# Two buffers for unpacked weights, the down unit's split one quad later on VectorE, and a four-step unpacking, in the first sweep of a 4-bit feed-forward kernel

## What is computed

```
x = layernorm(x + attention(x, w_qkv, w_o))      # 16 heads, causal
gate = x Wg^T ; up = x Wu^T                       # 4096 columns each
out  = (gelu(gate) * up) Wd^T
x = layernorm(x + out)
```

## Time and profile before

| | |
|---|---|
| median of 3 runs | 3083.97 us (3083.12 to 3085.64) |
| the profiled execution, its own time | 3093.57 us |
| its span, first to last instruction | 3091.8 us |
| PE busy, share of the span | 91% |
| DVE, ACT, POOL busy | 55%, 41%, 33% |
| mean granted TensorE clock | 0.961 of full speed |
| feed-forward phase | from about 911 us to the end |
| its first sweep | from about 937 us to about 1577 us |

### The profile page before, as it was taken

One profiled execution on the slowest core, in us unless ns is written; L12 is line 12 of the kernel. 1 busy time (PEld: TensorE's weight loads), 2 busy tenths in 40 slices (PEclk: granted clock), 3 DMA queues, 4 the chain that ended last, 5 costly groups with the idle time before them and its releaser, 6 DMA issues.

```text
span 3091.8 us, 42087 instructions
## 1 busy us (share of the span) xinstructions
PE 2798.1 (91%) x13314; PEld 2316.3 (75%) x13314; DVE 1700.2 (55%) x3645; ACT 1256.1 (41%) x2934; POOL 1017.6 (33%) x1112
## 2 busy tenths in 40 slices
PE   4999999999955888888889999999999999999997
PEld 3888788878843666666677888877888887788885
DVE  3887788778856667777743333334333334333333
ACT  3877777777743333333332222232222223222221
POOL 1433333334325555555542111132111114111112
PEclk9999999999987999999999999999999999999998
DMA  5566464656535444444445334354434353434341
GB/s 174 151 158 173 140 178 130 180 140 163 151 118 182 162 160 160 159 157 162 153 181 211 153 154 181 126 211 177 153 154 182 125 200 138 196 160 171 136 184 41
DMA packets 140012, 493.45 MB, mean 160 GB/s; under 512 B 11552, under 2 KB 44448, under 8 KB 115232
## 3 DMA queue, kind: packets, MB, share of 16 engines
q1 hardware_dynamic: 139808, 491.11, 46.2%
HBM read 356.84 MB, written 134.22 MB: 159 GB/s over the span
## 4 chain that ended last, share of the span: by engine, by line
PE 50%; DVE 9%; POOL 5%; DMA 3%; issue 2%; ACT 1%; SPq 0%; POOLq 0%; DVEq 0%; ACTq 0%
PE bank L906 17%; PE bank L907 16%; PE bank L908 16%; DVE bits_b L1158 2%; DMA wu<-w_scratch 2%; POOL wu L1321 1%; DVE w L1176 1%; DVE acc L1187 1%; POOL bx_l L1338 1%; DVE bits_a L1155 1%; POOL wu L1317 1%; DVE hid L1206 1%; ACT wu L1009 1%; DVE bits_a L1161 0%; DMA x_next<-x1T_scratch 0%
## 5 line engine op out<-in xcount | busy, mean ns | idle before, releaser
L1333 POOL TENSOR_TENSOR inter_l<-hid,inter_h 128x512 fp32r<-128x512 f32 x256 | 329.5, 1287 | 1194.4 <-ACT inter_h L1009 1194.4
L1187 DVE TENSOR_TENSOR acc<-acc,bank 128x512 f32<-128x512 f32 x512 | 347.9, 685 | 375.0 <-PE bank L908 366.3
L906 PE MATMUL bank<-wd,inter_h 128*128 128x512 f32 x1024 | 412.3, 403 | 62.6 <-DVE acc L1187 52.3
L682 POOL TENSOR_SCALAR probs<-probs,row_inv 128x128 f32<-128x128 f32 (+3 forms) x512 | 263.1, 533 | 537.1 <-DVE row_inv L602 537.1
L906 PE MATMUL bank<-bx_h,wu 128*128 128x512 f32 x896 | 359.9, 402 | 81.1 <-POOL wu L1321 71.7
L1206 DVE TENSOR_TENSOR hid<-hid,bank 128x512 f32<-128x512 f32 x192 | 131.8, 686 | 499.2 <-PE bank L908 462.8
L907 PE MATMUL bank<-wd,inter_h 128*128 128x512 f32 x1024 | 405.8, 396 | 0.0
L908 PE MATMUL bank<-wd,inter_l 128*128 128x512 f32 x1024 | 404.9, 395 | 0.0
L908 PE MATMUL bank<-bx_h,wu 128*128 128x512 f32 x896 | 357.4, 399 | 0.0
L907 PE MATMUL bank<-bx_l,wu 128*128 128x512 f32 x896 | 357.3, 399 | 0.0
L906 PE MATMUL bank<-bx_h,wg 128*128 128x512 f32 x896 | 353.1, 394 | 4.4 <-POOL wg L1321 2.6
(11 more groups left out here) (128 smaller groups left out, 5211.1 us busy)
## 6 DMA issues: line engine op xcount, KB each, us to landing
wg<-w_scratch SPq DMA_DIRECT2D x48, 1792.0 KB, 8.9
wu<-w_scratch SPq DMA_DIRECT2D x48, 1792.0 KB, 12.7
wd<-w_scratch SPq DMA_DIRECT2D x48, 1024.0 KB, 4.9
qk_scratch<-qk_stage SPq DMA_DIRECT2D x64, 512.0 KB, 2.9
q_st<-qk_scratch SPq DMA_DIRECT2D x128, 256.0 KB, 5.0
k_st<-qk_scratch SPq DMA_DIRECT2D x128, 256.0 KB, 7.1
w_scratch<-wg SPq DMA_DIRECT2D x16, 1792.0 KB, 5.9
w_scratch<-wu SPq DMA_DIRECT2D x16, 1792.0 KB, 5.7
```

Of the source, the lines that this page charges most:

```text
L682: pool.tensor_scalar(p, p, row_inv[:, h % 4, k:k + 1], 1.0, ALU.mult, ALU.mult).then_inc(norm_done, 1)
L906: pe.matmul(out, a(0), b(0), start=start, stop=False, skip_group_check=True)
L1187: dve.tensor_tensor(a, a, d_bank[n % 2][:, :], ALU.add).then_inc(d_added, 1)
L1333: pool.tensor_tensor(inter[1][:, m, t, :], hid[:, 2 * m + t, :], f32(inter[0][:, m, t, :]), ALU.subtract).then_inc(inter_split, 1)
```

## The change

It touches the first sweep alone. `w32` and `w_sum` become two buffers each (unit k takes `w32[k % 2]`; gate and up have a `w_sum` of their own), and `unpack_scale(k)` waits for the split of unit k - 2 instead of k - 1. `unpack_bits` takes four steps: one instruction shifts the codes by 12 and ors them with themselves, in place of a masked shift and a masked or. The down unit of quad j is no longer split at the end of quad j - 1 but in quad j, on ACT behind split_high(j - 1, 0, 1), and its low part is made by DVE, behind seed_e of u, with a semaphore of its own (`d_split`). `unpack_scale(k)` goes ahead of add 1, `unpack_bits(k + 1)` ahead of times_up(1,1), `unpack_scale(k + 1)` ahead of add 4. On ACT and POOL some steps change places. Cut to its core, `wait_split(eng, k)` being the wait for `d_split` or `gu_split` of unit k:

```diff
-    w32 = plan("w32", [P, 2, 512], F32)
-    w_sum = plan("w_sum", [P, 4, 2, P], F32)
-    plan("x_room", [P, 2048], F32)
+    w_sum = [plan("w_sum_g", [P, 4, 2, P], F32), plan("w_sum_u", [P, 4, 2, P], F32)]
+    w32 = [plan("w32_0", [P, 2, 512], F32), None]
+    plan("x_room", [P, 1024], F32)
+    w32[1] = plan("w32_1", [P, 2, 512], F32)
...
@@ SP
             for j in range(QUADS):
                 st, first = j // NG, j % NG == 0
-                if j + 1 < NG:
-                    for u in range(UNITS):
-                        k = UNITS * (j + 1) + u
-                        if k + 1 < UNITS * NG:
-                            load_unit(k + 1)
-                        if u:
-                            store_w(j + 1, u - 1)
-                    store_w(j + 1, 2)
-                elif j + 1 < QUADS:
+                if j < NG:
+                    for n in range(3):
+                        k = UNITS * j + 2 + n
+                        if k + 2 < UNITS * NG:
+                            load_unit(k + 2)
+                        if k < UNITS * NG:
+                            store_w(k // UNITS, k % UNITS)
+                if NG <= j + 1 < QUADS:
                     sp.wait_ge(prod_done, 14 * j)
                     load_w(j + 1, 0)
                     load_w(j + 1, 1)
...
                     if st == 0:
-                        sp.wait_ge(w_split, UNITS * NG)
+                        wait_split(sp, UNITS * NG - 2)
+                        sp.wait_ge(w_made, 2 * UNITS * NG)
...
@@ ACT, quad j
                 split_high(j - 1, 0, 1)
+                if j < NG:
+                    down_high(j)
+                take_u3(j, "g")
+                split_high(j, 0, 0)
                 if prep:
                     gate_up_high(j + 1, 0)
-                take_u3(j, "g")
-                split_high(j, 0, 0)
                 take_u3(j, "u")
-                gelu(j, 1, 1)
                 if prep:
                     sums_high(j + 1, 0)
+                gelu(j, 1, 1)
...
+                gelu(j, 1, 0)
                 if prep:
                     gate_up_high(j + 1, 1)
-                gelu(j, 1, 0)
...
-                if prep:
-                    sums_high(j + 1, 1)
                 split_high(j, 1, 0)
                 gelu(j, 0, 1)
+                if prep:
+                    sums_high(j + 1, 1)
...
-                if prep:
-                    down_high(j + 1)
@@ DVE
-                dve.tensor_scalar(bits_a[:, :], raw, 0xF0, 12, ALU.bitwise_and,
-                                  ALU.logical_shift_left).then_inc(bit_step, 1)
+                dve.scalar_tensor_tensor(bits_b[:, :], raw, 12, raw, ALU.logical_shift_left,
+                                         ALU.bitwise_or).then_inc(bit_step, 1)
                 dve.wait_ge(bit_step, step + 1)
-                dve.scalar_tensor_tensor(bits_b[:, :], raw, 0x0F, bits_a[:, :], ALU.bitwise_and,
-                                         ALU.bitwise_or).then_inc(bit_step, 1)
...
-                if k:
-
-                    dve.wait_ge(w_split, k)
+                if k >= 2:
+                    wait_split(dve, k - 2)
...
+            def down_low(j):
+                dve.wait_ge(w_high, 7 * j + 7)
+                dve.tensor_tensor(wd[j % 2][:, 1, :, :], w32[j % 2][:, :, :], f32(wd[j % 2][:, 0, :, :]),
+                                  ALU.subtract).then_inc(d_split, 1)
@@ POOL, quad j
                 if prep:
                     gate_up_low(j + 1, 0)
-                    sum_w(j + 1, 1)
...
                 if prep:
-                    gate_up_low(j + 1, 1)
+                    sum_w(j + 1, 1)
                 split_low(j, 1, 0)
...
                 if prep:
-                    down_low(j + 1)
+                    gate_up_low(j + 1, 1)
```

More of the change, by code:

```diff
@@ L792, in splitted, with wait_split @@
         return 4 * j + SPLIT.index((m, t)) + 1
+    def wait_split(eng, k):
+        j, u = k // UNITS, k % UNITS
+        if u == 2:
+            eng.wait_ge(d_split, j + 1)
+        else:
+            eng.wait_ge(gu_split, 2 * j + u + 1)
     def down_at(j, t, q):
@@ L1028, in gate_up_high @@
                     act.wait_ge(w_stored[u][j % 2], 16 * (j // 2))
-                copy(w[:, 0, 0:2, :, :], w32[:, :, :].rearrange("p e (c n) -> p e c n", c=2)[:, :, :, 0:P]).then_inc(w_high, 1)
-                copy(w[:, 0, 2, :, :], w32[:, 1, :].rearrange("p (c n) -> p c n", c=2)[:, :, P:GW]).then_inc(w_high, 1)
+                copy(w[:, 0, 0:2, :, :],
+                     w32[k % 2][:, :, :].rearrange("p e (c n) -> p e c n", c=2)[:, :, :, 0:P]).then_inc(w_high, 1)
+                copy(w[:, 0, 2, :, :],
+                     w32[k % 2][:, 1, :].rearrange("p (c n) -> p c n", c=2)[:, :, P:GW]).then_inc(w_high, 1)
             def sums_high(j, u):
@@ L1034, in sums_high @@
                 act.wait_ge(w_summed, 4 * (2 * j + u + 1))
-                copy(w[:, 0, 3:7, :, :], w_sum[:, :, :, :]).then_inc(w_high, 1)
+                copy(w[:, 0, 3:7, :, :], w_sum[u][:, :, :, :]).then_inc(w_high, 1)
             def down_high(j):
@@ L1041, in down_high @@
                     act.wait_ge(w_stored[2][j % 2], 16 * (j // 2))
-                copy(wd[j % 2][:, 0, :, :], w32[:, :, :]).then_inc(w_high, 1)
+                copy(wd[j % 2][:, 0, :, :], w32[j % 2][:, :, :]).then_inc(w_high, 1)
             def seed(j, x):
@@ L1116, in _ @@
                     x_part(st + 1, 4, x_next)
+                split_high(j, 1, 0)
+                gelu(j, 0, 1)
                 if prep:
                     sums_high(j + 1, 1)
-                split_high(j, 1, 0)
-                gelu(j, 0, 1)
                 if last:
@@ L1148, in unpack_bits @@
             def unpack_bits(k):
-                step = k * 5
+                step = k * 4
                 dve.wait_ge(unit_loaded[k % 2], 48 * (k // 2 + 1))
@@ L1300, in sum_w @@
             def sum_w(j, u):
-                n = 2 * j + u
-                pool.wait_ge(w_made, 2 * (UNITS * j + u + 1))
-                a = w32[:, :, :].rearrange("p e (c m n) -> p e m c n", c=2, m=2)
+                n, k = 2 * j + u, UNITS * j + u
+                pool.wait_ge(w_made, 2 * (k + 1))
+                if j:
+                    pool.wait_ge(gu_split, n - 1)
+                total = w_sum[u]
+                a = w32[k % 2][:, :, :].rearrange("p e (c m n) -> p e m c n", c=2, m=2)
@@ L1310, in sum_w @@
                 pool.wait_ge(w_summed, 4 * n + 3)
-                pool.tensor_tensor(w_sum[:, 3, :, :], a12, w_sum[:, 1, :, :], ALU.subtract).then_inc(w_summed, 1)
+                pool.tensor_tensor(total[:, 3, :, :], a12, total[:, 1, :, :], ALU.subtract).then_inc(w_summed, 1)
             def gate_up_low(j, u):
-                w = (wg, wu)[u][j % 2]
+                w, whole = (wg, wu)[u][j % 2], w32[(UNITS * j + u) % 2]
                 pool.wait_ge(w_high, 7 * j + 3 * u + 3)
-                pool.tensor_tensor(w[:, 1, 0:2, :, :], w32[:, :, :].rearrange("p e (c n) -> p e c n", c=2)[:, :, :, 0:P],
+                pool.tensor_tensor(w[:, 1, 0:2, :, :], whole[:, :, :].rearrange("p e (c n) -> p e c n", c=2)[:, :, :, 0:P],
@@ L1318, in gate_up_low @@
                                    f32(w[:, 0, 0:2, :, :]), ALU.subtract)
-                pool.tensor_tensor(w[:, 1, 2, :, :], w32[:, 1, :].rearrange("p (c n) -> p c n", c=2)[:, :, P:GW],
+                pool.tensor_tensor(w[:, 1, 2, :, :], whole[:, 1, :].rearrange("p (c n) -> p c n", c=2)[:, :, P:GW],
                                    f32(w[:, 0, 2, :, :]), ALU.subtract)
-                pool.tensor_tensor(w[:, 1, 3:7, :, :], w_sum[:, :, :, :], f32(w[:, 0, 3:7, :, :]),
-                                   ALU.subtract).then_inc(w_split, 1)
```

46 lines of the change are left out of this document (21 added, 25 removed).

## The result

| | before | changed |
|---|---|---|
| median, run in turns on the same chips | 3086.3 us (19 runs, 3082.54 to 3092.01) | 3099.9 us (19 runs) |
| ratio | | 1.0043, 95% interval 1.0034 to 1.0053 |
| the profiled execution, its own time | 3093.57 us | 3094.16 us |
| its span | 3091.8 us | 3092.4 us |

The change makes the kernel slower by 13.6 us. One disturbed run of 9389.53 us is left out of the ratio, as are one of e6 (7491 us) and one of e12 (3624 us) further down. The other 18 of the changed kernel lie between 3087.17 and 3115.58, three times as wide as those of before. The profiled execution of the changed kernel is 5.7 us under its median, that of before 7.3 above its own. So the two traces differ by 0.6 us only, and they are read for the parts.

A forecast was written before the change was run, and what follows sets the result against it. The first sweep was taken as bound by the cycle p1 u, c22, DVE's unpacking, POOL's sums and subtractions, p1 u. Quads +4, quad 0 -0.5, turn +16.2 gave +19.7 on 3083.97: 3103.7 us, range 3084 to 3118.

The forecast's parts named there:

- The turn: End of first sweep: quad 15's store of `wd` waits for `d_split`, delaying x of the next sweep; +16.2 us.
- First half of the cycle: From c22 of u to the scaled up unit on DVE, in turns with POOL: 0.5 us gained a quad.
- Second half: From scaled up unit to POOL's last subtraction: 10.2 us or 9.65 instead of 9.2, as DVE's down unit steps interleave.
- Edges of PE: PE's waits around p1 u: one 5 us gap inside the cycle costs nothing, down 0 waits less; 0.1 us gained a quad.
- The clock: Behind PE's gap ahead of p1 u: half clock for about 3.4 us, p5 u still 19.8 us behind p1 u.
- the cycles: The 14 cycles between quads 1 and 15 of the first sweep: +4 us in all, range -9 to +14.
- A: First sweep's quads: POOL and DVE do not meet, cycle 35.0 us, 3.7 less; 3048 us in all; chance 0.08.
- C: First sweep: the longer gap makes 7 more quads 1.0 us longer by half clock; 3111 us; chance 0.1.
- B: Second half only: down unit's codes land late, so DVE unpacks after POOL's chain; 3081 to 3094 us; chance 0.08.
- D: Turn of the sweep: the loads overtake and x is not late, only +3.5 us stays; 3087 us; chance 0.03.

The follow-up runs named there:

- e6: Kernel before with two `w32` buffers alone, the scaling waiting for the split of two units before: 3086.8 us, ratio 0.9999.
- e12: e11 with adds 6 and 7 also ahead of the down unit's scaling on DVE: 2987.07 us, ratio 0.9675.
- e1: Changed kernel with quad 15's store of `wd` issued behind the loads of x on SP: 3081.47 us, ratio 0.998.
- e3: e1 with the down unit's unpacking and scaling moved into the next quad, between add 0 and times_up(0,0): 3058.75 us, ratio 0.991.
- e7: e1 with the split of `hid` put back behind POOL's three subtractions of the up unit: 3067.71 us, ratio 0.9934.
- e5: e3 with the down unit's split and the up unit's bit steps and scaling ahead of c22 of u: 3040.34 us, ratio 0.9841.
- e10: e1 with DVE's order made new, down split and gate unit behind add 0, up unit's unpacking ahead of c22: 2996.97 us, ratio 0.9703.
- e11: e10 with add 1 ahead of the up unit's bit steps on DVE: 3010.46 us, ratio 0.9751.

## Why the prediction came out right

Forecast 3103.7, measured 3099.9; slower by 0.43%, forecast 0.64%. The change itself was forecast as +19.7 us and came out as +13.6; that the two times lie only 3.8 apart is in part luck, as the median of before came out 2.3 us higher than the 3083.97 that the forecast started from. Step by step:

- **The turn** was to cost 16.2 us. It cost 17.2 in the two traces, just above the 14 to 17 given for it, and e1 gets 18.4 back. The chain was as told: the store waits for `d_split`, made behind seed_e of u; x stands behind it on SP; no slack. x was used 42.5 us behind p1 u (1572.22 - 1529.75) where it had been 25.2.
- **First half of the cycle**: 0.5 less predicted, 0.38 measured (9.24 against 9.62, both from the start of c22 in the timeline). The turns came as worked out (L1166 1.22, L1169 2.51).
- **Second half**: 10.2 us predicted, 10.14 measured, against 9.23 before. That DVE's steps for the down unit would meet POOL's chain was the reason, and e3 takes just them away and gets 8.5. But one statement of this step was wrong: that the split of `hid` fills the pause and nothing is lost. e7 shows that it costs 0.87 us a quad, since DVE would have used the pause. The sum was right because the turns were counted one by one with the split in them.
- **Edges of PE**: one gap, the wait for `wu` longer: yes. DVE's wait for `w32` gone and worth nothing: yes, and e6 shows it alone. PE's waits for `wu`, "about 5 us each", are 3.64 ahead of the quads of 37.6 and of one of 39.2, and 5.24 ahead of the others but the first two.
- **The clock** is the term that failed, though it moved the sum little. I took the run-up from p1 u to c22 of u as fixed, 19.8 us at half clock behind the gap, and so +4 us over the quads. It was 18.05 in some quads and 20.87 in others, 19.22 on average over 14 quads against 20.30 before: -15.1 us. The two halves of the cycle, which were forecast well, make it about +7.5 (14 times 0.91 less 0.38). In the profiled execution the quads so came out 7.5 us shorter than before, not 4 longer, and many lie outside of the 38.6 to 39.8 us that were to show the forecast right. That the sum still held is luck in this term. In the median, with 17.2 for the turn and 0.4 for the start, what is left for the quads and the rest is 13.6 + 0.4 - 17.2 = -3.2 us. My range for the cycles, -9 to +14, held both. No experiment sets the phase by itself, so why it falls one way or the other in a quad stays open. It also explains, by argument only, why this kernel's runs scatter more than those of before.
- **Rivals.** A (the cycle gets short) fell: the profile has the instructions in turns. The buffer alone gave 0.9999 (e6). A's mechanism was sound, though: in e3 and e5, where DVE and POOL meet less, a quad takes 37.5 and 35.3 to 36.9. C (the clock costs more) went the other way in the traces, as told above. B (codes late) and D (x not late) did not come: DVE took the down unit's codes at 1173.18, right behind add 5.

The change's parts, if they add up: four steps -20, two buffers 0, the rest of the order in the quads about +15, of which e7 gives back 14, the turn +17 to +18. The first two are measured alone; the +15 is what is left.

## What to carry to other kernels

When a piece of work is moved later on one engine, look at every queue on which something waits for it, SP's above all: a store that waits in front of unrelated loads passes the whole delay on, here 17 us once, and one moved line gets it back. When two engines share a port, freeing one of them of work is no gain if the other's next work then falls into the critical chain: count the turns in the chain, not the busy times. And where a chain of waits is longer than the bounding engine's own work, look first at what stands in front of its first step only by the order of the stream: moving the unpacking ahead of c22 and filling DVE's waits took the quads from 39 to 31.65 us.

## What the runs showed of the hardware

**Turns, whole instructions each.** VectorE with two SBUF inputs of 512 columns took 0.69 us alone and from 1.04 to 2.78 beside GpSimd; GpSimd's 1024-column subtraction 2.34 alone (e3) and 2.57 to 2.84 beside VectorE; in none of these rows did one engine get two of its instructions in ahead of the other's. A tensor_scalar on int32 (0.43 alone, L1161 in the earlier trace rows; 2.51 as L1169 of the changed kernel at 1166.09) waits too, although it has one SBUF input. The Trainium skill (SBUF — State Buffer, "Who interferes with whom") says that whoever issues first keeps the shared ports for a whole instruction. The rows agree, and add that with both engines' next instruction ready the ports changed hands each time.

**The half clock need not follow the longest wait.** In the changed kernel it came behind a wait of 1.78 us (0.58 in the 4 us from 1172.40) and then not behind the one of 3.64 that followed (1.00 from 1182.00). In other quads of the same run it came behind the one of 5.24 (0.50 from 1259.30). Two waits of 1.5 and 1.6 us a quad (e10) left 1.00 over 296 us; one of 2.25, and 3.2 in two of eight quads (e11), left 0.95. So quads of one execution differed by up to 2.8 us (37.58 and 40.39) with the same work; ahead of the gap at 1181.76 the half clock cost nothing, since the gap was shorter by as much (3.64 against 5.24).
